# Attention on one core: context scores in a row among value steps, and a key projection behind the context shift's transpose

## The reference

```python
def _windowed_global_attention(q, k, v):   # 16 heads of 16, WINDOW 128, PREFIX 16
    ...
    scores = jnp.concatenate([jnp.where(mg[None, None], sg, neg), jnp.where(mt[None, None], st, neg)], axis=-1)
    attn = jax.nn.softmax(scores, axis=-1)
    ...
def _L0_xattn_ref(q, k, v, mask, Wq, bq, Wk, bk, Wv, bv, Wo, bo):
    ...
    scores = jnp.einsum('bhqd,bhkd->bhqk', qh, kh) / np.sqrt(D_K).astype(np.float32)
    scores = jnp.where(mask[:, None, :, :] == 0, jnp.float32(-1000000000.0), scores)
    probs = jax.nn.softmax(scores, axis=-1)
    ctx = jnp.einsum('bhqk,bhkd->bhqd', probs, vh)
    ...
x = x + _L0_attn_ref(_layernorm(x, axis=-1), L0_attn_w_qkv, L0_attn_w_out)
x = x + _L0_xattn_ref(_layernorm(x, axis=-1), ctx_1024, ctx_1024, mask_BxSxS2_if1, ...)
x = x + _L0_ffn_ref(_layernorm(x, axis=-1), ...)
```

## Time and profile before

| | us |
|---|---|
| median of 3 runs | 1151.12 |
| lowest, highest | 1147.78, 1152.88 |
| profiled execution | 1152.57 |
| its span, first to last instruction | 1150.8 |
| TensorE busy | 1069.2 (93%) |
| VectorE busy | 725.1 (63%) |
| ScalarE busy | 476.8 (41%) |
| GpSimd busy | 496.4 (43%) |

### The profile page before, as it was taken

One profiled execution on the slowest core, in us unless ns is written; L12 is line 12 of the kernel. 1 busy time (PEld: TensorE's weight loads), 2 busy tenths in 40 slices (PEclk: granted clock), 3 DMA queues, 4 the chain that ended last, 5 costly groups with the idle time before them and its releaser, 6 DMA issues. The chain is left out here.

```text
span 1150.8 us, 28853 instructions
## 1 busy us (share of the span) xinstructions
PE 1069.2 (93%) x9838; PEld 710.7 (62%) x9847; DVE 725.1 (63%) x2088; ACT 476.8 (41%) x869; POOL 496.4 (43%) x744
## 2 busy tenths in 40 slices
PE   8999899999999999999989899999989999999994
PEld 3546455565464564554645446666648999999962
DVE  4655776767757767677563544777774555565554
ACT  5435545454545454544444223433213333333351
POOL 3324525335244243252442131545363566666654
PEclk9999999999999999999999999999998999999998
DMA  7283563744644737537357335364213111111100
GB/s 224 71 214 91 145 191 99 197 132 128 186 117 120 193 99 193 144 103 196 96 137 205 90 115 172 124 188 145 94 57 98 57 55 55 53 55 51 54 26 8
DMA packets 143724, 137.53 MB, mean 120 GB/s; under 512 B 31641, under 2 KB 136991, under 8 KB 143521
## 3 DMA queue, kind: packets, MB, share of 16 engines
q1 hardware_dynamic: 137824, 123.72, 38.5%
q0 software_dynamic: 4992, 12.66, 3.3%
q10 hardware_dynamic: 832, 0.16, 0.1%
HBM read 48.50 MB, written 50.43 MB: 86 GB/s over the span
## 5 line engine op out<-in xcount | busy, mean ns | idle before, releaser
L980 ACT ACTIVATE probs<-ps_ab 128x512 f32<-128x512 f32 (+2 forms) x352 | 175.0, 540 | 86.0 <-PE ps_ab L1301 36.6
L600 POOL TENSOR_SCALAR_AFFINE_SELECT probs<-probs 128x512 f32<-128x512 f32 x128 | 83.3, 651 | 259.0 <-ACT probs L980 254.6
L3105 PE MATMUL ps_ab<-e_yT,e_w_now 128*128 128x128 f32 x1024 | 121.7, 278 | 0.0
L3105 PEld LDWEIGHTS ps_ab<-e_yT,e_w_now 128*128 128x128 f32 x1024 | 118.8, 195 | 0.4 <-ACT e_yT L3006 0.4
L3116 PE MATMUL ps_c<-keep_w,e_hT 128*128 x512 | 115.9, 379 | 0.0
L3116 PEld LDWEIGHTS ps_c<-keep_w,e_hT 128*128 128x128 f32 x512 | 94.8, 190 | 12.4 <-issue 0.8
L721 DVE CUSTOM_DVE_ANT_0 ps_ab<-ps_ab,mask_qk 128x256 f32<-128x256 f32 x224 | 89.2, 450 | 14.8 <-PE ps_ab L1271 14.6
L715 DVE TENSOR_REDUCE top<-ps_ab 128x2 f32<-128x512 f32 (+1 forms) x112 | 74.1, 683 | 26.1 <-PE ps_ab L1271 24.4
L1271 PE MATMUL ps_ab<-k_rows,q_rows 96*128 96x256 bf16 (+1 forms) x512 | 84.5, 260 | 6.2 <-DVE top_prefix L707 2.9
L3006 ACT ACTIVATE e_yT<-ps_d 128x256 f32<-128x256 f32 x36 | 13.8, 383 | 151.8 <-PE ps_d L3056 151.8
L1858 ACT ACTIVATE e_w_now<-keep_w 128x1024 f32 x64 | 64.1, 1049 | 30.1 <-DVE m_rows_upto_all L2450 20.1
(11 more groups left out here) (290 smaller groups left out, 2169.6 us busy)
## 6 DMA issues: line engine op xcount, KB each, us to landing
sorted_rows<-filler SPq DMA_DIRECT2D x8, 4290.0 KB, 18.1
q_rows<-parts SPq DMA_DIRECT2D x96, 128.0 KB, 2.4
k_rows<-parts SPq DMA_DIRECT2D x96, 128.0 KB, 2.4
q_rows<-q_parts SPq DMA_DIRECT2D x96, 128.0 KB, 2.4
keep_w<-in_e_w SPq DMA_DIRECT2D x16, 512.0 KB, 4.7
keep_w<-in_e_w SPq DMA_DIRECT2D x8, 1024.0 KB, 8.4
e_row<-sorted_rows SPq DMA_DIRECT2D x32, 130.0 KB, 2.1
x_in<-in_x SPq DMA_DIRECT2D x8, 512.0 KB, 4.1
```

The source lines that it names most:

```text
L600: nc.gpsimd.affine_select(own, own, [[0, TILES], [1, P]], ALU.is_ge, keep_zero, base=0, channel_multiplier=-1).then_inc(probs_cut.sem, 1)
L980: nc.scalar.activation(probs[:, user % 2, lo:lo + width], ps_exp[:, f % 2, 0:width], ACT.Exp).then_inc(exp_done.sem, 1)
L3105: mm = nc.tensor.matmul(ps_h[s][:, f // 4, (f % 4) * P:(f % 4 + 1) * P], w1_now[:, s, k, f * P:(f + 1) * P], yT[:, s, k * P:(k + 1) * P], ...
```

## The change

Only the order of instructions changes, and with it the list of the work banks.

- TensorE: in passes with cross-attention the first two late fills go from behind the fourth window step to behind the heads' transposes, ahead of the feature transposes. The first context fill goes in among the value steps, the "shiftB" transpose ahead of the last value step. The other context fills follow each other, since the key projection j = 3 leaves its two places among them (where it stood in halves); the first two window steps of group 2 go among the last context fills and ahead of the first early fill; "shiftT2" stands behind that fill, then a second early fill, then the whole projection. In pass 0 the projection goes behind the sums' transposes.
- ScalarE: the shift copy and its two DMA issues go ahead of `group_sums(n, 1)` and of `middle_part(n, 2)`; `high_part(n, 3)` and `middle_part(n, 3)` go around the exponentials of step 2, behind the context shift's copy.
- VectorE: `split_rest(n, (3,))` goes behind three early maxima (in pass 0 behind `normalise_heads(n, 1)`).
- GpSimd: the last low part goes behind the masks of group 2.

```diff
-         "q1", "shiftB", "k1", "s1", "shiftT2", "s2", "shiftA", "ctxT", "k2", "v2", "out2_0", "out2_1", "v0", "v1"]
+         "q1", "shiftB", "s1", "shiftT2", "k1", "s2", "shiftA", "ctxT", "k2", "v2", "out2_0", "out2_1", "v0", "v1"]
...
                     if front:
-                        low_parts(n, range(2, 4))
+                        low_parts(n, (2,))
                     cut_group(n, 2)
+                    if front:
+                        low_parts(n, (3,))
...
-                    if front:
-                        split_rest(n, (3,))
-                    if cross:
-                        context_maxima(n, range(TILES, TILES + 2))
+                        context_maxima(n, range(TILES + 2))
...
-                    if front:
+                    if front and cross:
+                        early_maxima(n, range(3))
+                        split_rest(n, (3,))
+                        early_maxima(n, range(3, 13))
+                    elif front:
+                        split_rest(n, (3,))
                         early_maxima(n, range(13))
...
                     if cross:
                         heads_transposes(n)
+                        late_scores(2)
...
-                    late_scores(2)
+                    if not cross:
+                        late_scores(2)
...
                     group_sums(n, 0)
                     if front:
                         high_part(n, 2)
-                    group_sums(n, 1)
-                    if front:
-                        middle_part(n, 2)
                     shift_rows(n, "shiftB", shiftT[1], shiftT_ready)
                     ...
+                    group_sums(n, 1)
                     if front:
+                        middle_part(n, 2)
+                    if front and not cross:
                         high_part(n, 3)
                         middle_part(n, 3)
                     probs_claim(n, user_window(n, 2))
                     head_exps(n, 2, 0)
+                    if front:
+                        head_exps(n, 2, 1)
                     if cross:
                         shift_rows(n, "shiftT2", shiftT2, shiftT2_ready)
-                    for j in range(1, GROUP + 1):
+                    if front and cross:
+                        high_part(n, 3)
+                        head_exps(n, 2, 2)
+                        middle_part(n, 3)
+                    for j in range((3 if cross else 2) if front else 1, GROUP + 1):
                         head_exps(n, 2, j)
...
+                    if cross:
+                        context_scores(n, 0, (0,))
                     shift_transposes(n, "shiftB", shift[1], shift_ready, shift_ready.count(n, 2))
+                    window_values(n, 1, GROUP)
+                    if cross:
+                        context_scores(n, 0, (1, 2, 3))
+                        context_scores(n, 1, (0,))
                     sums_transposes(n, 1)
...
+                        context_scores(n, 1, (1,))
+                        window_shifted(n, 2, 0)
+                        context_scores(n, 1, (2, 3))
+                        window_shifted(n, 2, 1)
+                        early_scores(1)
+                        shift_transposes(n, "shiftT2", shift2, shift2_ready, shift2_ready.count(n, 1))
+                        early_scores(1)
+                        queries_or_keys(n, 3)
+                        window_shifted(n, 2, 2)
+                        early_scores(1)
```

More of the change, by code:

```diff
@@ L896, in iteration @@
                     if cross:
-                        context_maxima(n, range(TILES))
-                    if front:
-                        split_rest(n, (3,))
-                    if cross:
-                        context_maxima(n, range(TILES, TILES + 2))
+                        context_maxima(n, range(TILES + 2))
                     normalise_heads(n, 1)
@@ L1631, in iteration @@
                         queries_or_keys(n, 2)
-                    for j in range(2, GROUP + 1):
+                    for j in range(2, GROUP):
                         window_values(n, 1, j)
                         late_scores(1)
+                    if cross:
+                        context_scores(n, 0, (0,))
                     shift_transposes(n, "shiftB", shift[1], shift_ready, shift_ready.count(n, 2))
+                    window_values(n, 1, GROUP)
                     if cross:
-                        context_scores(n, 0, range(2))
-                    if front:
-                        queries_or_keys(n, 3, (0,))
-                    if cross:
[L1641 to L1649, removed]
+                        context_scores(n, 0, (1, 2, 3))
+                        context_scores(n, 1, (0,))
+                    sums_transposes(n, 1)
+                    if last:
+                        context_scores(n, 1, (1, 2, 3))
+                        return
+                    if cross:
+                        context_scores(n, 1, (1,))
[8 more added lines that the diff above has]
+                        early_scores(1)
                     else:
+                        queries_or_keys(n, 3)
                         keep_warm(ps_out[:, 1, :], 6)
@@ L1654, in iteration @@
                         early_scores(2)
[L1655 to L1661, removed]
+                        window_shifted(n, 2, 0)
+                        early_scores(1)
+                    for j in range(3 if cross else 1, GROUP + 1):
                         window_shifted(n, 2, j)
```

## The result

The changed kernel took **1162.31 us** (median of 7 runs, 1157.42 to 1166.2), the kernel before in the same series 1151.12 (1147.78 to 1153.55): ratio 1.0087, 95% interval 1.0063 to 1.011. It is slower by 0.9%. The forecast was 1158 and slower, with 1157 to 1161 as its main case and a range up to 1163. A second series of the same changed kernel (6 runs, further down) gave 1159.43 against 1152.33, ratio 1.0072 (1.0044 to 1.01).

What follows compares the result with a forecast made beforehand. TensorE, busy almost without a break, bounds the kernel, so its waits decide: +1.5 (pass 0), +1.0 + 2.2 (pass 1), +2.75 (passes 2 to 6), -0.5 (pass 7) make +6.95 us, put at a median of 1158 us, range 1150 to 1163.

Steps and rivals of the forecast that it cites:

- main case: Whole kernel: slower, at 1157 to 1161 us, given a chance of 0.5.
- Sum: Whole kernel: the terms of pass 0, pass 1, passes 2 to 6 and pass 7 together cost +6.95 us.
- Late fills before the features, passes 2 to 7: Head of the pass: two late fills cover TensorE's 0.42 us idle before the feature transposes, gaining 0.5 us a pass.
- Pass 1's head: First late fill: TensorE waits 1.4 us for the upper key rows from SyncE, so the pass loses 1.0 us.
- The context part, passes 2 to 6: Waits for the rows' DMA at the first early fill and ScalarE's exponentials at step 4: loss of 1.05 us a pass.
- Pass 1's context part: First early fill to first shifted context scores: 7.35 us instead of 5.17, a loss of 2.2 us.
- Pass 0: Key projection behind the sums' transposes no longer covers ScalarE's work: loss of 1.5 us, with a 1.9 us wait.
- Pass 7: Gains 0.5 us at its head; its shift transposes wait for VectorE and an unmoved DMA: 0.
- Closing part: End of the kernel: no term of its own in the forecast's sum, so no gain or loss.
- The rival on the clock: TensorE's longer wait before pass 1's early fill drops its clock: 1159.5 to 1167 us; with a further wait, chance 0.08.
- The rule on transfers: First early fill: the moved projection uncovers the rows' DMA wait; rows in time would make the sum 2 us lower.

Runs made afterwards that it cites:

- s3: The changed kernel measured once more, unaltered, on the chip of the spare-product runs: 1159.43 us against 1152.33 before, ratio 1.0072.
- e4: Changed kernel plus five throwaway matrix products on TensorE ahead of the first early fill, in its wait for the rows: 1161.02 us, ratio 1.0107 to before.
- s1: Changed kernel plus four throwaway matrix products on TensorE ahead of window step 4 in passes 1 to 6: 1160.36 us, ratio 1.0084 to before.
- e1: Kernel before with only the first two late fills moved ahead of the feature transposes: 1149.34 us against 1150.95, ratio 0.9982.
- e2: Changed kernel with only the late fills' move undone, leaving the context part and pass 0's new order: 1161.38 us, ratio 1.01 to before.
- r1: Changed kernel with the early fills' last two row transfers issued by ScalarE instead of SyncE in passes 1 to 6: 1161.69 us, ratio 1.0081 to before.
- e3: Changed kernel with window step 3's exponentials ahead of the key part's middle step on ScalarE: 1153.3 us, ratio 1.0028 to before.
- r2: Changed kernel with pass 0 alone back in the order of before on every engine: 1158.22 us, ratio 1.0048 to before.
- r4: Changed kernel with step 3's exponentials moved forward, ScalarE issuing the last two row transfers, and pass 0 as before: 1148.59 us, ratio 0.9973 to before.
- s2: Changed kernel plus throwaway matrix products at both waits, five at the first early fill and four ahead of step 4: 1160.47 us, ratio 1.0069 to before.

## Why the prediction was right, and where its sizes were off

**Sum.** Forecast +6.95 us. At equal clock the changed kernel is 7.4 us slower than before in the series that had both (s3), and the trace's attention part is 8.19 longer, of which 1.7 is the fall in pass 1: 6.5. The traces of e4 and s1, the same order without a fall, give 5.9 and 6.1. The sum was right: by the traces 0.5 to 1 too high, by the fit within its error. By parts, forecast and trace: pass 0 1.5 and 1.7, pass 1 3.2 and 3.1 without its fall, passes 2 to 6 2.75 and 2.0, pass 7 -0.5 and -0.3. It did not contain the clock's some 2 us; sum and clock together give 9.1 on 1151.12, 1160.2. The 13 runs of both series have a mean of 1160.8. The first series' median, 1162.31, lies beyond the 1157 to 1161 of the forecast's main case and near the range's end; the second's, 1159.43, lies inside. Which side a median of six or seven runs comes out on is chance.

**Late fills before the features, passes 2 to 7.** Forecast 0.5 us a pass, with 0.4 to 0.55 as its bounds. It was 0.7 in passes 2 to 6 of the trace (the period grew by 0.40, with 1.11 lost in the context part), 0.31 in pass 7, 0.6 in e1. Mis-sized by 0.2 a pass. The wait at the features (0.42) is gone as said. The step that was mis-sized is the idle time that the fills cover: 0.42 is counted from the modelled end of the heads' transposes, which stands 0.16 late. From start to start these take 0.90 us (337.81 to 338.71) when the fills follow, and 1.48 (330.56 to 332.04) stood there before: 0.58 to be had and not 0.42. With the feature transposes 0.05 shorter (0.88 against 0.93) the gain at the head of pass 4 is 0.63 us in the trace of after; the other 0.07 come behind the context part. The heads' transposes before,

```profile
330.56 1.06 PE L1361 MATMUL ps_d<-identf,heads_out 128*128 128x128 f32 x8
```

and after, with the first late fill behind them:

```profile
337.81 1.06 PE L1370 MATMUL ps_d<-identf,heads_out 128*128 128x128 f32 x8
338.71 0.38 PE L1275 MATMUL ps_ab<-mask_qk,ident 128*128 128x512 bf16 x1
```

**Pass 1's head.** Forecast a wait of 1.4 and a loss of 1.0; the trace of after has 1.94 and 1.49. SyncE's last issue stands there at 100.04 against 97.88, 2.16 later, while TensorE's heads' transposes moved by 1.68. But this is one execution: in s3, the same kernel, the wait is 1.26 and the loss 0.8, and over the eight traces with this head and with pass 0 as changed the waits are 1.17 to 1.94, 1.45 on the mean. So the forecast was right here; one trace alone would have said that it was not. The fill in s3:

```profile
102.01 0.39 PE L1275 MATMUL ps_ab<-mask_qk,ident 128*128 128x512 bf16 x1 [1.26 <-DMA k_rows<-parts]
```

**The context part, passes 2 to 6.** Forecast 1.05 us a pass, measured 1.11 in the trace and 1.06 in e2. This part of pass 4 begins 6.62 us later than before (7.25 at the heads' transposes, less 0.63 won at the head). With these taken off, the fill comes at 369.28 (forecast 369.25), step 4 at 375.57 (375.5), the first shifted context scores at 376.68 (376.6). VectorE's shift is ready at 369.24 (369.1), 1.4 us sooner than before, and brings nothing, as said. The two waits are 1.34 and 1.07 where about 1.2 and 1.25 were said. That the rows' DMA and not VectorE sets the fill's start is shown by r1, and that the key part's chain through ScalarE sets step 4's by e3.

**Pass 1's context part.** Forecast 2.2; measured 3.3 with the fall in it, 1.6 without. The wait for the rows is 2.88 instead of nearly 4; in the traces of this order that leave it alone it is 2.88 to 3.88 (s3 3.08, s1 3.24, e3 3.88), so one execution settles its size to 1 us only. s1, without a fall, has 2.0.

**Pass 0.** Forecast 1.5 and a wait of 1.9; measured 1.68 and 1.86; undone in r2 it gave 1.47 back. **Pass 7.** Forecast -0.5, measured -0.31. Closing part: 0 as said.

**The rival on the clock** was given 0.08, as a case of its own beside the sum. That was the mistake that cost most: by the pooled clocks it doesn't stand beside the forecast, it comes on top of it. The fall happened where it was named, in pass 1, in the changed kernel's trace and in those of e2, e3, r1 to r4, s2 and s3; not in those of e4 and s1, though s1 waits 3.24 us there. The Trainium skill's rule on it ("TensorE: Matmul & The Clock Gate", HAM oscillation), that waits for DMA between groups of matmuls bring back the lower clock, is borne out as to direction by the row at 142.50. Its remedy there is an order of the loop in which the array stays busy; spare products in the waits, which are not that, brought nothing in e4, s1 and s2.

**The rule on transfers** ("DMA: Bandwidth & Descriptors", Rules for kernel authors, in the Trainium skill): issue early and wait late. The trace agrees: uncovering the wait for the rows cost it 1.34 us in pass 4. The price that can be had back is smaller, though: in r1, with 0.4 won there, it is VectorE's shift again that holds the transpose behind it.

**The later stages.** The trace of after is 3.3 us shorter there. It has three stretches of half clock between 660 and 1140 us, 10.2 us in all, where the trace of before has four, 17.1 us in all, in the same code. 6.9 us less at half clock are 3.4 us of time by the price of a fall. So single traces compare to within 3 us only, and a change of the attention part is best read up to its own end.

**What would beat both.** r4, with the change's order, its two waits treated and pass 0 left alone, took 0.9973 (0.9955 to 0.999) of the kernel before. e1, the late fills alone, took 0.9982 (0.9964 to 0.9999). By these intervals they are not told apart: the context part of the change, with all its repairs, adds at most a few tenths of a per cent to what two moved lines give.

## What to carry to other kernels

When work is moved away from in front of a wait, list everything that the engine will then meet next, DMA landings above all, and cost the new place by the latest of them; the wait that the profile shows is only the one that ended last. When a chain that crosses engines is moved into a stretch of short steps, look at each queue that it enters for what stands directly behind it: here one exponential placed ahead of a middle part was worth 0.9 us a pass. And on a kernel whose clock falls and recovers, fit time against clock over the runs before putting small differences down to instructions.

## What the runs showed of the hardware that I had not expected

Two issuing engines did not bring the rows sooner in proportion: 1.1 us of earlier issue became 0.4 us of earlier landing, the time to landing rising from 2.5 to some 3.1 us. Time follows the run's mean granted clock closely, 0.97 us for each 0.001, with a remainder of 1.3 us: three quarters of the variance of one kernel's runs go with the clock. And TensorE running spare products in a wait left the clock of the runs as it was (.9871 in 19 runs, .9868 in all with the wait).
